# One change in three places of a two-layer attention and expert kernel: a product moved to GpSimd, feature products rewritten as row-block pairs, and a new table of steps

## Chip, cores, metric

The kernel runs on one core of one Trainium2 chip. The metric is the device time of one execution in microseconds (us). In the profile, PE is TensorE (PEld its weight loads), DVE is VectorE, ACT is ScalarE, POOL is GpSimd and SP is SyncE, which issues the DMAs.

## What is computed

Four batches of 512 tokens, width 128, go through two post-norm layers, every step with a residual and a layer norm behind it:

```python
x = ln(x + softmax_attention(x))              # layer 1: 16 heads of 8, rotary positions
# layer 1, experts: 16 experts of 64, 4 of them per token, and a shared one of 128
g = silu(einsum('th,efh->tef', x, w1_e)); u = einsum('th,efh->tef', x, w3_e)
x = ln(x + einsum('tef,ehf,te->th', g * u, w2_e, combine) + swiglu_shared(x))
# layer 2, attention: linear, with features
q, k, v = x @ Wq + bq, x @ Wk + bk, x @ Wv + bv            # 16 heads of 8
q_prime = (elu(einsum('bhsd,dm->bhsm', q, random_matrix)) + 1) / 16    # m = 32
k_prime = the same of k
x = ln(x + (q_prime (k_prime' v) / (q_prime sum(k_prime))) @ Wo + bo)
x = ln(x + x @ W.T + b + low_rank_experts(x))    # layer 2: 8 experts of rank 16, 2 per token
```

## The kernel before

Everything is float32 but the scores of layer 1. The program is written out by hand for each engine (`nc.Block()`), with semaphores; all engines walk through the same lists of steps, each taking its own part of a step (`beside_pe`, `beside_act`, `beside_dve`, `beside_pool`). An engine runs its instructions in order, so a wait on one holds all that stands behind it.

**Attention of layer 1** comes first (to about 268 us), with the steps of `slots` between its 128 half tiles. Step `combine` of batches 0 and 1 makes the tokens' expert weights `wT` and SP stores them to DRAM (`store_weights`, L358); SP brings them back spread over partitions, one tile `cw` (128x512) per pair of experts, into three buffers (`load_weights`, L362). The first `load_weights` is issued when SP has gone through all of `slots` (L402).

**The expert loop** (L778 on PE, L910 on ACT, L1248 on DVE) has 36 iterations: for each batch eight pairs of experts (p = 0 to 7) and the shared expert (p = 8, `EP`). Iteration i does on PE a `gate_e` and an `up_e` product of 128x512 (L784), then the `down` products of iteration i-1 (four of 128x128, L771), which add up over a batch in one PSUM bank. Between them ACT makes tanh of the gate (L915), DVE makes silu's product (L1254) and the product with up (`prod`, L956 from L1265), and DVE then multiplies by the expert weights `cw` into `hid` (L956 from L1270). PE waits for `hid` before `down`.

**Layer 2 beside the loop.** The list `beside[i]` holds the steps that each engine does in iteration i: PE does the first of them before `down(i-1)` and the others behind it (L785 to L791). What the loop has no room for is `layer2`, the list behind it. `chunk` sums the expert output, `norm1` normalises, `x2T` transposes; `K` and `Q` make feature blocks, `V` the values, `KV` the sums over tokens, `O`, `OT` the output, `AT` and `Y1` the projection, `norm2`, `x3T`, `lg` (gates and low-rank products), `ghT`, `Y2`, `norm3` the last part. Batch n enters the table at iteration 9(n+1), so batch 3 lies wholly in `layer2`.

**K and Q features.** Because q and k go at once through the random matrix, the products Wq·R and Wk·R (`rbd` is the random matrix repeated on the diagonal, 128x512) are made once, in steps `wR`, and their bias rows in `kb`. A bias row is split into three bf16 parts by five DVE instructions (L1146 to L1152) and laid on three partitions by three DMAs (L406). A `K` or `Q` step of one block (four of each per batch) is then one float32 product of 128x512 (L658, L664) and a bf16 product of three rows that adds the bias (L659, L665). ACT makes exp of the result less 1 (L867, L873; bias `minus1`), and DVE takes max(min(exp, 1), result) from there, with the result read from PSUM (L1159, L1175).

**Chains on DVE** (statistics, routing, low-rank gates) are generators; `step(n)` runs n of their links between other work, three (`step(1)`, `step(2)`) and `step(3)` in an expert iteration, and `finish` runs what is left before a step that needs it. GpSimd does the two small instructions of each norm's deviation (L448, L449) and adds bias rows to the residual (L454); it has no part in the loop's own work.

## Time and profile before

| | us |
|---|---|
| median of 3 runs | 527.77 (526.52 to 531.72) |
| the profiled execution | 527.63 |
| its span, first to last instruction | 525.8 |
| PE busy / weight loads | 481.0 / 232.8 |
| DVE busy | 386.0 |
| ACT busy | 224.6 |
| POOL busy | 106.5 |

Busy time is the union of an engine's instructions. A matmul's recorded end contains the run through the array, so records of PE overlap: how long a product holds PE is read from the distance between starts. A float32 product has two records and two weight loads. Many groups share L956, DVE's helper for two-input instructions, or L426, GpSimd's; they are told apart by tiles. In the trace `QS` and `KS` are also the memory of `gate_s`, `prod`, `hid` and of the exponentials (they lie over the score tiles), and `probs` that of the feature weights.

### The profile page before, as it was taken

Reading aid. Unit: us, or ns where it says so; the run is one execution under the profiler, and the core shown is the slowest. Engines: PE = TensorE matmul, PEld = TensorE weight load, DVE = VectorE, ACT = ScalarE, POOL = GpSimd, SP = SyncE. Lnnn points to the kernel's source line nnn. Section 1 sums busy time; section 2 is a strip of 40 time slices with the busy share of each in tenths; the row PEclk is TensorE's granted clock in tenths of the full one; section 3 lists DMA queues with packets and bytes.
Section 4 is the critical chain, followed back from the end, with each engine's and each line's share of the span. In section 5 each row is a group of like instructions: output and inputs, shape, how many; then the busy total and the mean of one; then the engine's idle time right before and its main releaser. Section 6 shows DMA issues by size and latency. Waiting matters only on the chain. (4 is left out here: it accounts for less than half of the span.)

```text
span 525.8 us, 7943 instructions
## 1 busy us (share of the span) xinstructions
PE 481.0 (91%) x2903; PEld 232.8 (44%) x2903; DVE 386.0 (73%) x994; ACT 224.6 (43%) x302; POOL 106.5 (20%) x101
## 2 busy tenths in 40 slices
PE   8889899999999999989979979999999999988772
PEld 3333233334333343333335545556557456545471
DVE  6398888887898888798629796974678466655553
ACT  2306657667766656656841222231332232233110
POOL 9880427006440010000100002000011001212020
PEclk9999999999999999999999999998999799879756
DMA  4854342224322333200132113112111000000000
GB/s 155 259 142 156 90 123 92 91 70 112 115 91 70 93 86 113 66 1 22 23 80 82 60 42 100 42 60 60 41 42 51 30 20 1 21 1 0 22 20 20
DMA packets 24878, 36.31 MB, mean 69 GB/s; under 512 B 2684, under 2 KB 16258, under 8 KB 24834
## 3 DMA queue, kind: packets, MB, share of 16 engines
q1 hardware_dynamic: 24840, 35.81, 23.3%
q8 instruction: 23, 0.38, 0.3%
q14 instruction: 15, 0.12, 0.1%
HBM read 24.07 MB, written 11.53 MB: 68 GB/s over the span
## 5 line engine op out<-in xcount | busy, mean ns | idle before, releaser
L1092 DVE TENSOR_REDUCE negmax<-psum 128x1 f32<-128x512 f32 x256 | 169.6, 687 | 34.0 <-PE psum L521 33.8
L805 ACT ACTIVATE probs<-psum 128x1024 f32<-128x1024 f32 x128 | 127.7, 1022 | 60.1 <-PE psum L537 57.7
L521 PE MATMUL psum<-KS,QS 125*128 125x512 bf16 x256 | 98.5, 385 | 7.4 <-DVE negmax L1092 4.1
L556 PE MATMUL psum<-probs,VA 128*32 128x256 f32 x1024 | 80.5, 390 | 0.4 <-ACT probs L805 0.4
L537 PE MATMUL psum<-QS,KS 128*128 128x512 bf16 x256 | 76.0, 380 | 0.1
L784 PE MATMUL psum<-xT,late 128*128 128x512 f32 x144 | 73.3, 634 | 0.0
L521 PEld LDWEIGHTS psum<-KS,QS 125*128 125x128 bf16 x256 | 24.5, 96 | 82.0 <-DVE negmax L1092 39.9
L448 POOL TENSOR_SCALAR var<-mv 128x4 f32<-128x4 f32 x16 | 4.3, 270 | 262.6 <-DVE mv L992 262.5
L915 ACT ACTIVATE QS<-psum 128x512 f32<-128x512 f32 x36 | 21.5, 597 | 65.2 <-PE psum L784 65.2
L771 PE MATMUL psum<-late,QS 128*128 128x128 f32 x288 | 40.6, 285 | 5.7 <-DVE QS L956 3.0
L1254 DVE SCALAR_TENSOR_TENSOR QS<-QS,psum 128x512 f32<-128x512 f32 x36 | 24.5, 680 | 26.1 <-ACT QS L915 26.1
L771 PEld LDWEIGHTS psum<-late,QS 128*128 128x128 f32 x288 | 35.9, 193 | 16.3 <-DVE QS L956 9.0
L556 PEld LDWEIGHTS psum<-probs,VA 128*32 128x32 f32 x1024 | 20.8, 108 | 38.1 <-issue 27.6
L784 PEld LDWEIGHTS psum<-xT,late 128*128 128x128 f32 x144 | 26.1, 201 | 21.4 <-issue 20.9
L537 PEld LDWEIGHTS psum<-QS,KS 128*128 128x128 bf16 x256 | 23.3, 99 | 20.1 <-issue 2.9
L426 POOL TENSOR_TENSOR res<-res,late 128x512 f32<-128x512 f32 x12 | 15.7, 1312 | 75.0 <-ACT xT L847 75.0
L426 POOL TENSOR_TENSOR rot<-rot,early 128x512 f32<-128x512 f32 x12 | 15.3, 1274 | 73.2 <-ACT rot L828 72.7
L712 PE MATMUL psum<-warm_in 128*128 128x512 bf16 x91 | 26.6, 410 | 1.5 <-POOL warm_in L478 1.5
L956 DVE TENSOR_TENSOR QS<-QS,cw 128x512 f32<-128x512 f32 x32 | 22.5, 704 | 3.8 <-DMA cw<-w_dram 3.3
L956 DVE TENSOR_TENSOR QS<-QS,psum 128x512 f32<-128x512 f32 x32 | 21.8, 683 | 2.1 <-PE psum L784 0.6
L867 ACT ACTIVATE KS<-psum,minus 128x512 f32<-128x512 f32 x16 | 11.0, 688 | 27.2 <-PE psum L659 27.2
L1175 DVE SCALAR_TENSOR_TENSOR QS<-KS,psum 128x512 f32<-128x512 f32 x16 | 10.9, 684 | 13.2 <-ACT KS L873 13.2
(148 smaller groups left out, 590.0 us busy)
## 6 DMA issues: line engine op xcount, KB each, us to landing
stack_dram<-parts SPq DMA_DIRECT2D x24, 384.0 KB, 3.3
cw<-w_dram SPq DMA_DIRECT2D x32, 256.0 KB, 3.3
KS<-stack_dram SPq DMA_DIRECT2D x16, 288.0 KB
QS<-stack_dram SPq DMA_DIRECT2D x16, 288.0 KB
late<-in_late SPq DMA_DIRECT2D x8, 346.5 KB, 4.4
res<-in_x SPq DMA_DIRECT2D x4, 256.0 KB, 3.3
w_dram<-wT SPq DMA_DIRECT2D x4, 256.0 KB, 4.4
out_y<-KS SPq DMA_DIRECT2D x4, 256.0 KB, 2.2
```

What stands on the lines that cost most here:

```text
L426: return nc.gpsimd.tensor_tensor(out=o, in0=a, in1=b, op=op)
L521: mm(sm_bank(u)[:, :], QS[b % 2][0:KROW, h, qt * P:(qt + 1) * P], KS[b % 2][0:KROW, h, :], start=True, stop=True).then_inc(sm_full, 1)
L537: last_ = mm(ps[2 * hf + j][:, :], KS[b % 2][0:KROW + 3, h, kt * P:(kt + 1) * P], QS[b % 2][0:KROW + 3, h, :], start=True, stop=True)
L556: last_ = mm(ps[6][32 * j:32 * j + 32, q], VA[b % 2][:, kt, h, :], probs[:, n % 2, j, q], start=(kt == 0 and half == 0), stop=(kt == NT - ...
L712: mm(ps[6][:, :], warm_in[:, 0:P], warm_in[:, :], start=True, stop=True)
L771: last_ = mm(bank_of(u)[:, t * D:(t + 1) * D], hid[:, i % 3, t * P:(t + 1) * P], w2, start=(p == 0 and t == 0), stop=(p == EP and t == NT ...
L784: mm(bank_of(u)[:, :], wt, xT[:, b * T:(b + 1) * T], start=True, stop=True).then_inc(fullness(u), 1)
L805: fn(probs[:, n % 2, 2 * hf:2 * hf + 2, :], psum[:, 2 * hf:2 * hf + 2, :], ACT.Exp, scale=float(DH) ** -0.5).then_inc(exp_done, 1)
L915: fn(gate_s[:, i % 2, :], bank_of(u)[:, :], ACT.Tanh, scale=0.5).then_inc(tanh_done, 1)
L956: return V.tensor_tensor(out=o, in0=a, in1=b, op=op)
L1092: V.tensor_reduce(out=negmax[:, G % 4, i:i + 1], in_=sm_bank(u)[:, :], axis=X, op=ALU.max, negate=True).then_inc(sm_free, 1)
L1254: V.scalar_tensor_tensor(out=h_, in0=h_, scalar=1.0, in1=bank_of(g)[:, :], op0=ALU.add, op1=ALU.mult)\
```

## The change

- **Experts**: `hid = prod * cw` of the 32 routed pairs is done by GpSimd, in a loop over the 36 iterations that it now walks in order with its other steps. `hid_done` is split: `routed_done` (GpSimd) and `shared_done` (DVE). DVE's `step(2)` goes with the product.
- **Features**: `wR`, `kb`, their DMAs and the bf16 bias products go. New steps `kp` and `qp`, once per batch, make the projections kT and qT (one 128x512 product each; ACT copies them to SBUF and adds the bias). A feature block then contracts over a block of heads only: K as products of 256 columns over 64 rows, Q as products of 512 columns over 32 rows, with two blocks issued together, each on its own rows of the array (`tile_position`). ACT does two instructions per block, exp and result + 1, both to SBUF, and frees the PSUM bank; DVE reads both from SBUF.
- **Table**: one list `steps`, the same for all batches, with up to 24 iterations from `chunk` to `norm3`, in place of `a_round`; what lies past iteration 35 is `layer2`, later batches first within an iteration's place.
- **Weights**: the first three `load_weights` are issued straight behind the store of batch 0 (slot 112 of 128).

The places of the steps in the new table, by iteration (batch behind the name): 0 gate2; 1 to 4 heads3; 5 attnT3; 6 proj3; 8 norm3 combine2; 9 chunk0; 10 resT3 norm1_0; 13 gate3 x2T0; 14 kp0 qp0; 15 K0 pair; 16 K0 pair, V0; 17 Q0 pair; 18 chunk1, Q0 pair, KV0; 19 O0; 20 combine3, OT0; 21 AT0; 22 x2T1; 23 kp1 qp1 Y1_0; 24 K1 pair; 25 K1 pair, V1; 26 Q1 pair, x3T0; 27 Q1 pair, KV1, lg0; 28 O1; 29 OT1; 30 AT1 ghT0; 31 x2T2 Y2_0; 32 kp2 qp2 Y1_1; 33 K2 pair; 34 K2 pair, V2; 35 Q2 pair, x3T1. Behind the loop: chunk3, Q2 pair, KV2, lg1, norm1_3, O2, OT2, AT2, ghT1, x2T3, Y2_1, kp3, qp3, Y1_2, norm3_1, K3 pair, norm2_2, K3 pair, V3, Q3 pair, x3T2, Q3 pair, KV3, lg2, O3, OT3, AT3, ghT2, Y2_2, Y1_3, norm3_2, norm2_3, x3T3, lg3, ghT3, Y2_3, norm3_3.

```diff
@@ steps beside the loop
+        steps = ((0, "chunk", 0), (1, "norm1", 0), (4, "x2T", 0), (5, "kp", 0), (5, "qp", 0), (6, "K", 0), (6, "K", 1),
+                 (7, "K", 2), (7, "K", 3), (7, "V", 0), (8, "Q", 0), (8, "Q", 1), (9, "Q", 2), (9, "Q", 3), (9, "KV", 0),
+                 (10, "O", 1), (10, "O", 0), (11, "OT", 1), (11, "OT", 0), (12, "AT", 0), (14, "Y1", 0), (15, "norm2", 0),
+                 (17, "x3T", 0), (18, "lg", 0), (21, "ghT", 0), (22, "Y2", 0), (23, "norm3", 0))
+        for n in reversed(range(NB)):
+            for at, kind, c in steps:
+                beside[PAIRS * (n + 1) + at].append((kind, n, c))
@@ when a PSUM bank is free
-                    "kb": (row_done, c + 1), "Q": (qf_done, 4 * b + c + 1), "K": (kf_done, 4 * b + c + 1),
+                    "Q": (expq_done, 4 * b + c + 1), "K": (expk_done, 4 * b + c + 1),
@@ SP
                     if kind == "combine":
                         store_weights(a)
+                        if a == 0:
+                            for j in range(CW):
+                                load_weights(j)
-            for j in range(NB * EP):
-                if j == 12:
-                    sp.wait_ge(kb_done, 2)
-                    for i in range(3):
-                        sp.dma_start(bias_stack[i:i + 1, :, :], bias_parts[0:1, :, i, :]).then_inc(ks_ld, 16)
+            for j in range(CW, NB * EP):
@@ GpSimd
+            for i in range(NB * PAIRS):
+                b, p = divmod(i, PAIRS)
+                if p < EP:
+                    j = b * EP + p
+                    pool.wait_ge(prod_done, j + 1)
+                    pool.wait_ge(cw_ld[j % CW], 16 * (j // CW + 1))
+                    if i >= 3:
+                        pool.wait_ge(down_done, i - 2)
+                    tt(hid[:, i % 3, :], prod[:, j % 2, :], cw[:, j % CW, :], ALU.mult).then_inc(routed_done, 1)
+                for s in beside[i]:
                     beside_pool(*s)
@@ PE
+                if kind in ("kp", "qp"):
+                    last_ = mm(o[:, :], c_["wk1" if kind == "kp" else "wq1"], xT[:, b * T:(b + 1) * T], start=True, stop=True)
                 if kind == "K":
-                    mm(o[:, :], tile_of(m), wkR[:, :], start=True, stop=False)
-                    last_ = mm(o[:, :], onesb[:, 0:P], bias_stack[:, 0, :], start=False, stop=True)
+                    other = ("K", b, m + 1)
+                    wait_free(pe, other)
+                    for t in range(2):
+                        for r, out_ in enumerate((o, bank_of(other))):
+                            half = slice(64 * r, 64 * (r + 1))
+                            last_ = mm(out_[:, 256 * t:256 * (t + 1)], kT[half, (m + t) * P:(m + t + 1) * P],
+                                       c_["rbd"][half, 256 * r:256 * (r + 1)], start=True, stop=True,
+                                       tile_position=(64 * r, 0))
                 if kind == "Q":
-                    mm(o[:, :], wqR[:, m * P:(m + 1) * P], xT[:, b * T:(b + 1) * T], start=True, stop=False)
-                    last_ = mm(o[:, :], bias_stack[:, 1, m * P:(m + 1) * P], onesb[:, :], start=False, stop=True)
+                    other = ("Q", b, m + 1)
+                    wait_free(pe, other)
+                    for c, out_ in ((m, o), (m + 1, bank_of(other))):
+                        rows_ = slice(HW * c, HW * (c + 1))
+                        last_ = mm(out_[:, :], c_["rbd"][rows_, c * P:(c + 1) * P], qT[rows_, :], start=True, stop=True,
+                                   tile_position=(HW * c, 0))
@@ down
-                pe.wait_ge(hid_done, i + 1)
+                pe.wait_ge(*((shared_done, b + 1) if p == EP else (routed_done, b * EP + p + 1)))
@@ ACT (Q the same with eq_, qone, qT)
+                if kind == "kp":
+                    wait_full(act, u)
+                    if a:
+                        wait_full(act, ("K", a - 1, 3))
+                    fn(kT, bank_of(u)[:, :], ACT.Identity, bias=c_["bk_col"]).then_inc(kT_done, 1)
                 if kind == "K":
...
-                    fn(ek_[:, i % 2, :], bank_of(u)[:, :], ACT.Exp, bias=minus1[:, 0:1]).then_inc(expk_done, 1)
+                    fn(ek_[:, i % 2, :], bank_of(u)[:, :], ACT.Exp)
+                    fn(kone[:, i % 2, :], bank_of(u)[:, :], ACT.Identity, bias=plus1[:, 0:1]).then_inc(expk_done, 1)
@@ DVE, an expert iteration
-                    tt(prod[:, i % 2, :], h_, bank_of(u)[:, :], ALU.mult).then_inc(prod_done, 1)
-                    step(2)
-                    dve.wait_ge(prod_done, b * EP + p + 1)
                     j = b * EP + p
-                    dve.wait_ge(cw_ld[j % CW], 16 * (j // CW + 1))
-                    tt(hid[:, i % 3, :], prod[:, i % 2, :], cw[:, j % CW, :], ALU.mult).then_inc(hid_done, 1)
+                    if j >= 2:
+                        dve.wait_ge(routed_done, j - 1)
+                    tt(prod[:, j % 2, :], h_, bank_of(u)[:, :], ALU.mult).then_inc(prod_done, 1)
                 step(3)
```

## Rows read from the trace of the kernel before

**Rows 1.** Busy time by stretch: window, PE, PEld, DVE, ACT, POOL, clock, DMA.
```profile
267.80:445.20 177.40, 167.42 (x785) 98.62 (x783) 127.24 (x340) 48.68 (x81) 13.85 (x16) 0.97 0.19 53
445.20:495.00 49.80, 43.73 (x238) 25.14 (x238) 27.68 (x110) 13.68 (x23) 8.76 (x11) 0.86 0.04 11
495.00:525.80 30.80, 16.43 (x72) 14.30 (x70) 14.78 (x69) 3.21 (x6) 4.99 (x7) 0.56 0.06 18
```

**Rows 2.** Groups by line, the expert loop alone: shapes, count, busy, mean, idle before.
```profile
L784 PE MATMUL psum<-xT,late 128*128 128x512 f32 x144 | 73.3, 634 | 0.0
L771 PE MATMUL psum<-late,QS 128*128 128x128 f32 x288 | 40.6, 285 | 5.7 <-DVE QS L956 3.0 <-DVE z L956 2.6
L956 DVE TENSOR_TENSOR QS<-QS,cw 128x512 f32<-128x512 f32 x32 | 22.5, 704 | 3.8 <-DMA cw<-w_dram 3.3
```

**Rows 3.** Waits of the loop, weight loads: us in total, times, longest.
```profile
PEld psum L771 <- DVE QS L956: 9.0, 6, 3.6
```

**Rows 4.** Timeline: an iteration with a Q step (start, duration; then a line).
```profile
345.74 1.02 PE L664 MATMUL psum<-xT,probs 128*128 128x512 f32 x2
...
346.70 0.39 PE L665 MATMUL psum<-onesb,probs 3*128 3x512 bf16 x1
347.01 0.97 PEld L771 LDWEIGHTS psum<-late,QS 128*128 128x128 f32 x8 [0.23 <-issue]
...
348.01 1.88 PE L784 MATMUL psum<-xT,late 128*128 128x512 f32 x4
```

**Rows 5.** Timeline: iterations 3 and 4 on PE, with a heads step each.
```profile
279.89 1.88 PE L784 MATMUL psum<-xT,late 128*128 128x512 f32 x4
...
283.35 1.88 PE L784 MATMUL psum<-xT,late 128*128 128x512 f32 x4
```

**Rows 6.** Timeline: the first product with a weight tile.
```profile
274.35 0.69 DVE L956 TENSOR_TENSOR QS<-QS,cw 128x512 f32<-128x512 f32 x1 [3.31 <-DMA cw<-w_dram]
...
275.10 1.16 PE L771 MATMUL psum<-late,QS 128*128 128x128 f32 x8 [2.74 <-DVE QS L956]
```

**Rows 7.** Timeline: the second bias row on DVE, and iteration 10 behind it.
```profile
307.04 0.68 DVE L1146 TENSOR_SCALAR probs<-psum 128x512 f32<-128x512 f32 x1
...
309.37 0.68 DVE L956 TENSOR_TENSOR probs<-probs 1x512 bf16<-1x512 f32 x1
...
312.87 0.97 PEld L771 LDWEIGHTS psum<-late,QS 128*128 128x128 f32 x8 [2.82 <-DVE QS L956]
```

**Rows 8.** Timeline: tanh, the two DVE products and an exp, iteration 18.
```profile
345.08 0.60 ACT L915 ACTIVATE QS<-psum 128x512 f32<-128x512 f32 x1 [0.37 <-PE psum L784]
...
345.71 0.69 DVE L1254 SCALAR_TENSOR_TENSOR QS<-QS,psum 128x512 f32<-128x512 f32 x1 [0.28 <-ACT QS L915]
...
346.49 0.69 DVE L956 TENSOR_TENSOR QS<-QS,psum 128x512 f32<-128x512 f32 x1
...
347.12 0.69 ACT L873 ACTIVATE KS<-psum,minus 128x512 f32<-128x512 f32 x1 [1.44 <-PE psum L665]
```

**Rows 9.** Timeline: GpSimd's 128x512 instructions beside DVE's with two SBUF inputs.
```profile
320.91 0.69 DVE L956 TENSOR_TENSOR QS<-QS,cw 128x512 f32<-128x512 f32 x1
320.93 1.80 POOL L426 TENSOR_TENSOR res<-res,late 128x512 f32<-128x512 f32 x1 [3.77 <-ACT xT L847]
...
393.77 1.27 POOL L426 TENSOR_TENSOR res<-res,late 128x512 f32<-128x512 f32 x1 [10.42 <-ACT xT L847]
...
394.28 1.31 DVE L956 TENSOR_TENSOR QS<-QS,cw 128x512 f32<-128x512 f32 x1
```

**Rows 10.** Timeline: eight records of four column tiles (L674), between other products.
```profile
361.22 1.06 PE L784 MATMUL psum<-xT,late 128*128 128x512 f32 x1
362.21 1.06 PE L674 MATMUL psum<-QS,KVB 128*32 128x512 f32 x8
363.21 1.16 PE L771 MATMUL psum<-late,QS 128*128 128x128 f32 x8
```

**Rows 11.** Timeline behind the loop: first step, KV of batch 2, attention's end in batch 3.
```profile
445.26 0.60 PE L646 MATMUL psum<-early,res 128*128 128x128 f32 x4
...
450.13 3.76 PE L669 MATMUL psum<-VK,KS 128*128 128x33 f32 x32
...
494.01 0.69 DVE L956 TENSOR_TENSOR attn<-psum,rt 128x512 f32<-128x512 f32 x1
```

More of the change, by code:

```diff
@@ L208, in program @@
             slots[32 * last + at].append((kind, b, 0))
-        beside = [[] for _ in range(NB * PAIRS + 12)]
+        beside = [[] for _ in range(NB * PAIRS + 25)]
         for at, kind, b, i in ((0, "gate", 2, 0), (1, "heads", 3, 0), (2, "heads", 3, 1), (3, "heads", 3, 2), (4, "heads", 3, 3),
-                               (5, "wR", 0, 0), (5, "attnT", 3, 0), (6, "wR", 0, 1), (6, "proj", 3, 0), (7, "kb", 0, 0),
-                               (8, "norm", 3, 0), (8, "combine", 2, 0), (8, "kb", 0, 1), (10, "resT", 3, 0),
+                               (5, "attnT", 3, 0), (6, "proj", 3, 0),
+                               (8, "norm", 3, 0), (8, "combine", 2, 0), (10, "resT", 3, 0),
@@ L221, in program @@
-        round_at = (4, 4, 5, 5, 5, 6, 6, 7, 7, 7, 8, 8, 9, 9, 9, 10, 10, 11, 12, 12, 12, 12)
-        for n in range(NB):
-            w = PAIRS * (n + 1)
-            for at, kind in ((0, "chunk"), (1, "norm1"), (3, "x2T")):
-                beside[w + at].append((kind, n, 0))
-            if n + 1 < NB:
-                for (kind, back, c), at in zip(a_round, round_at):
-                    if n >= back:
-                        beside[w + at].append((kind, n - back, c))
+        steps = ((0, "chunk", 0), (1, "norm1", 0), (4, "x2T", 0), (5, "kp", 0), (5, "qp", 0), (6, "K", 0), (6, "K", 1),
[3 rows of a table added]
@@ L230, in program @@
+        for n in reversed(range(NB)):
+            for at, kind, c in steps:
+                beside[PAIRS * (n + 1) + at].append((kind, n, c))
         layer2 = [s for one in beside[NB * PAIRS:] for s in one]
         del beside[NB * PAIRS:]
-        crowded = {s for one in beside for s in one} | set(layer2)
-        for n in range(last, NB + 2):
-            layer2 += [(kind, n - back, c) for kind, back, c in a_round if 0 <= n - back < NB]
+        crowded = {s for one in beside for s in one}
@@ L237, in program @@
         uses = [[] for _ in range(8)]
-        in_misc = ("rope", "val", "max", "heads", "attnT", "proj", "resT", "gate", "combine", "wR", "kb", "x2T")
+        in_misc = ("rope", "val", "max", "heads", "attnT", "proj", "resT", "gate", "combine", "x2T")
         uses[MISC] = [s for one in [[("val", 0, 0), ("max", 0, 0)]] + slots for s in one if s[0] in in_misc]
@@ L246, in program @@
             uses[5].append(("y_e", b, 0))
-        bank_for = {"K": 2, "Q": 0, "V": 4, "KV": 5, "O": 5, "OT": 5, "AT": 7, "Y1": 4, "x3T": 7, "lg": 5, "ghT": 7, "Y2": 6, "x2T": 7}
+        bank_for = {"kp": 3, "qp": 1, "K": 2, "Q": 0, "V": 4, "KV": 5, "O": 5, "OT": 5, "AT": 7, "Y1": 4, "x3T": 7, "lg": 5, "ghT": 7, "Y2": 6, "x2T": 7}
         swap = 0
@@ L502, in _ @@
                     add_row("bout_row", 0, w // 32)
-            for one in beside + [layer2]:
-                for s in one:
+            for i in range(NB * PAIRS):
[8 more added lines that the diff above has]
+                for s in beside[i]:
                     beside_pool(*s)
+            for s in layer2:
+                beside_pool(*s)
         @block.tensor
```

92 lines of the change are left out of this document (40 added, 52 removed).

## The prediction

> **What bounds the kernel now.** I read the busy time by stretch first. The kernel has three parts: attention until 267.8 us, which the change leaves as it is but for the place of three DMAs; the expert loop, 177.4 us, with PE busy for 167.4 of them; and what lies behind the loop, 80.6 us, where PE is busy for 60.2 and the granted clock falls to 0.86 and then 0.56 [rows 1]. So the loop is bound by PE's own work and the last part by a chain that goes round all engines.
>
> The groups of the loop and the timeline say what an iteration costs PE. Two float32 records of 512 columns take 1.02 us and four take 1.88 [rows 4], so each further record is 0.43 and a product of 512 columns holds PE for 0.86. `down` holds it for 0.89 (1.00 where a bf16 product stands ahead: 347.01 to 348.01 [rows 4]). An iteration with nothing beside it is therefore 1.72 + 0.89 = 2.6 us, and 36 of them are 94. I priced each step beside the loop in the same way: four transposes 0.45, eight records of 128 columns 0.9, `KV` 3.7 [rows 11], a Q or K block 1.27 (345.74 to 347.01 [rows 4]). All of it with the 36 iterations makes 155 us. The other 22 are stalls and low clock: the wait for the first weight tile (2.74), the wait behind the second bias row (2.82), DVE being late in iterations 2 to 5, the clock after the `KV` steps. The waits name DVE: PE's weight loads of `down` waited 9.0 us for it [rows 3], and an early iteration with a `heads` step takes 3.46 us [rows 5] where PE's own work is 3.0.
>
> **The change, part by part**, against the profiled execution of 527.6 us (span 525.8 and 1.8 around it; the median of the runs is 0.1 above it).
>
> *Weight tiles sooner.* DVE got its first tile at 274.35 after a wait of 3.31, and PE waited 2.74 for `down(0)` [rows 6]. The store and three loads now pass SP some 15 slots earlier, behind the last load of maxima that attention needs, so they hold up nothing; what SP then waits for is only the second `combine`. The stall goes; late next is `hid` of iteration 0 by GpSimd, about when PE comes to it. **-2.7**, bounds 0 and -3.5.
>
> *Feature steps in the loop.* 22 blocks at 1.27 go (27.9). In their place come 6 projections at 0.86 (5.2) and 11 pairs. No row has two row blocks side by side. The nearest are the column tiles: four products of 512 columns, eight records, hold PE from 362.21 to 363.21, 1.00 us, where one after the other would be 3.43; about 0.14 of it is the change to the tiled form, and as much stands ahead of it [rows 10]. If two row blocks overlap like this, a pair is 0.86 + 0.28 = 1.14; if not, 1.72 + 0.28 = 2.00. These are the bounds; I take 1.14, because the column tiles are the nearest row. 11 pairs are 12.5, and 27.9 - 5.2 - 12.5 = 10.2 saved. `x3T` of batch 1 moves into the loop, 0.45. **-9.8**, bounds -0.3 and -9.8.
>
> The Trainium skill has a rule that speaks against it: TensorEngine Tiling (Array Packing), section Key Properties, says that a change of tiling mode drains the engine. By that rule each pair pays at both ends; the trace agrees, with the 0.14 us on either side, and it is small beside the 1.4 us that a pair saves. The page TensorE: Matmul & The Clock Gate, Part 3, gives 3.07 times for four row tiles of K = 32, by which a pair would be near its lower bound; no run here shows that yet.
>
> *`wR` and `kb` gone.* Four products, 4 x 0.86, in iterations where PE had no slack: **-3.4**. On DVE each `kb` is five instructions, for the second one 307.04 to 310.05, 3.0 us, and behind it stands the wait of 2.82 in iteration 10 [rows 7]. That stall goes, though norm and the sum of batch 0 remain at that place: **-2.5**, bounds 0 and -3.5.
>
> *`x2T` one iteration later.* It stood behind a normalisation still under way; one more iteration covers it. **-1.0**, bounds 0 and -1.5.
>
> *The product on GpSimd.* DVE loses 32 instructions, 22.5 us busy [rows 2]. GpSimd's instruction of this shape with two SBUF inputs takes 1.27 [rows 9] where DVE's takes 0.69. In a bare iteration PE comes to `down(i)` 0.86 (up) + 0.89 + 1.72 = 3.5 us after the end of its gate product. The chain is 0.60 tanh, 0.69, 0.69 [rows 8], then 1.27, and some 0.1 at each of four handoffs: 3.65. So bare iterations lose 0.1 to 0.3, and those with a step beside them (29 of 36) nothing, if DVE comes in time. DVE comes sooner than before, since it was the late one in iterations 2 to 5: **-1.5** there. Against it stand the feature pairs: ACT now does four instructions of 0.60 to 0.69 [rows 8] per pair ahead of the next tanh, 2.6 us, and the next `hid` is ready some 6.0 us after the pair ends, where PE needs it after 4.3 + the step beside it (1.1 or more), or 7 where the pair stands first in its list. GpSimd takes its place in the table's order too: a deviation waits behind the product, and the product behind a bias row that waits for `x2T`; both are 1.3 us against a period of 4. I put all these new stalls at **+3**, bounds 0 and +32 (1 us for each product).
>
> *Behind the loop.* DVE's attention output of batch 3 ends at 494.7, 49.5 us after the loop's last `down` [rows 11]. Laying the new list end to end from that `down`: Q pair and `KV` of batch 2 to 5.0, `lg` 6.9, `O` and `OT` 10.1, `AT` 11.8. Then `ghT` of batch 1 waits: its gates' chain has 16 links, about 4.5 us of DVE, and the list gives it only the eight of `OT` ahead of a `finish`, so PE stands until about 16.5. `Y2`, `kp`, `qp`, `Y1` to 22.2; the K pairs at the pace of ACT (four blocks x 1.3 = 5.2), the Q pairs the same, `KV` from 33.5 to 37.2, `lg`, `O`, `OT`, and the output at 43.5. PE has more holes there than before, so I add 2 for the clock (0.86 there now [rows 1]): 45.5, -4. At the end `Y2` of batch 2 stands ahead of `Y1` of batch 3, +1.9, but the normalisation of batch 2 no longer waits beside batch 3's `lg`, -1.4. Together **-3.5**, bounds -9 and +5.
>
> Sum: -2.7 - 9.8 - 3.4 - 2.5 - 1.0 - 1.5 + 3.0 - 3.5 = -21.4, so **506.2 us**.
>
> **Rivals.**
> - *Row blocks one after the other.* For it: no row shows row tiles. Against: column tiles overlap in full. 0.86 more for each of 11 pairs in the loop, 9.5; behind the loop ACT covers all but about 1.5. 506.2 + 11 = 517.
> - *ACT or DVE takes over in feature iterations, and the clock falls with PE's thinner work.* For it: DVE's work there (two products, two maxima, ten links) is about 4.6 us against 3.7 to 4.5 of PE, and low clock is seen wherever PE streams few columns ([rows 1], last row). 0.5 us in a dozen iterations is 6, or three or four more low stretches: 512.
> - *GpSimd's product and DVE shut each other out: slower.* Where both have two SBUF inputs, DVE's product of 394.28 took 1.31 instead of 0.69, ending 0.55 after GpSimd's, and GpSimd's of 320.93 took 1.80 behind DVE's of 320.91 [rows 9]. The new product starts right behind `prod`, just where DVE goes on with links, and its maxima now have two SBUF inputs. DVE's busy time in the loop, 127.2 less 22.5 and 5.8 for `kb`, is 99; shut out for 1.27 by each of 32 products it would be 140, as much as PE's, and the two would wait in turn. It decides from 0.67 us per product (21.4 / 32), above the +3 taken; at 1.0 per product (32 - 3 = 29) the time is 535. Against: most of what DVE does behind `prod` waits for ACT anyway, and its two products read PSUM. The Trainium skill, SBUF — State Buffer, Who interferes with whom, calls this an exclusive lock for the whole instruction; the trace agrees, with the two rows named.
> - *More stalls go than I count*: of the 22 us some 12 I keep; half of them gone is 500 or less.
>
> **How the numbers follow.** Forecast 0.52 (its own range 501 to 512), ACT, DVE or clock 0.17, row blocks in turn 0.14, fewer stalls 0.10, shut out 0.07. About 1%, 5 us, is what a measurement of this kernel can tell from no change. 495 to 521 reaches over the faster case and that of the rows in turn and leaves out the slower one and the outer ends. Faster by over 1% (below 522.5) takes all but the slower case and a part of the second and third: 0.88; within 1% 0.05; slower 0.07.
>
> **What would show it.** In the profile after: no DVE wait on DMA for `cw` and `down(0)` near 272; pairs of K or Q at 1.1 to 1.2 us from start to start of what is around them (2.0 if in turn); the GpSimd product at 1.3, over 1.6 on average if shut out; the loop at 159 to 161 us and 75 to 79 behind it; PE waiting for `ghT` of batch 1 some 4 us. A loop over 170 us with PE waiting for GpSimd's product at `down` would prove the forecast wrong.

## The result, and the profile after

| | before | after |
|---|---|---|
| median | 527.77 us (20 runs, 523.61 to 531.72) | 532.66 us (20 runs, 528.73 to 536.15) |
| ratio | | 1.0108, 95% interval 1.0079 to 1.0136 |
| profiled execution / its span | 527.6 / 525.8 | 536.15 / 534.4 |
| mean granted clock of the span | 0.952 | 0.909 |

The changed kernel is 1.1% slower. The forecast was 506.2 us, so 26 us are missing. The profiled execution is the slowest of the 20, 3.5 us above the median, so its stretches are somewhat long. Medians in this document are over all runs of a kernel, while ratios leave out runs more than 1.5% above its fastest, so that the ratio of e6 rests on two of its six runs.

Busy time by stretch, with the columns of [rows 1] (window, PE, PEld, DVE, ACT, POOL, granted clock, DMA), says in which half. These are the loop and what lies behind it:

```profile
271.40:437.00 165.60, 157.11 (x794) 100.94 (x792) 118.53 (x307) 61.03 (x108) 54.61 (x50) 0.94 0.18 53
437.00:534.40 97.40, 63.89 (x306) 48.34 (x304) 41.38 (x169) 22.10 (x41) 12.27 (x16) 0.64 0.03 9
```

Against [rows 1], the loop is 11.8 us shorter (177.4 to 165.6; forecast 159 to 161). What lies behind it is 16.8 us longer (80.6 to 97.4; forecast 75 to 79). The granted clock there fell from a mean of 0.75 to 0.64. The attention in front is 3.5 us longer (267.8 to 271.3). Its own steps are not edited, and it took 268.2 to 271.1 in the kernels below, with and without the early weight loads, so nothing shows that this is part of the change.

The groups and waits of the changed kernel. First the page's group of the product on GpSimd, then two groups of the stretch behind the loop (count, busy us, mean ns, idle before), then a wait of the loop (us in total, times, longest):

```profile
L410 POOL TENSOR_TENSOR QS<-QS,cw 128x512 f32<-128x512 f32 x32 | 40.8, 1274 | 111.5 <-DVE QS L977 109.6
...
L680 PE MATMUL psum<-VK,KS 128*128 128x33 f32 x64 | 11.5, 354 | 0.0
...
L711 PE MATMUL psum<-early,KS 128*128 128x128 f32 x12 | 2.9, 385 | 9.4 <-DVE KS L977 9.4
...
PEld psum L782 <- POOL QS L410: 6.3, 8, 1.5
```

GpSimd's product takes 1.27 us each, as forecast, and is rarely shut out. PE's weight loads of `down` wait 6.3 us for it, where they waited 9.0 for DVE [rows 3]. The trouble is behind the loop: `KV` took 11.5 us for two batches (7.5 before), and `ghT` (L711) waits 9.4 us for DVE (2.6 before). PE's timeline of that stretch:

```profile
437.08 1.13 PE L672 MATMUL psum<-probs,late 32*128 32x512 f32 x4
438.14 4.50 PE L680 MATMUL psum<-VK,KS 128*128 128x33 f32 x32
443.31 1.85 PE L697 MATMUL psum<-late,xT 128*128 128x8 f32 x8 [0.67 <-DVE KVB L977]
...
446.99 3.64 PE L685 MATMUL psum<-QS,KVB 128*32 128x512 f32 x16
...
458.75 1.11 PE L711 MATMUL psum<-early,KS 128*128 128x128 f32 x4 [4.41 <-DVE KS L977]
...
480.36 7.04 PE L680 MATMUL psum<-VK,KS 128*128 128x33 f32 x32
...
502.19 1.12 PE L711 MATMUL psum<-early,KS 128*128 128x128 f32 x4 [3.42 <-DVE KS L977]
...
515.35 1.11 PE L643 MATMUL psum<-early,res 128*128 128x128 f32 x4 [5.93 <-DVE res L1021]
```

`KV` of batch 3 is 32 records as in [rows 11], where it took 3.76 us; here it takes 7.04. The low-rank gates (L697) and `O` (L685) take 1.85 and 3.64; at full clock the same sets take 1.04 and about 1.9 in runs below. The wait for `ghT` of batch 1 is 4.41, which the forecast had (4). It did not have that for batch 2 (3.42), nor 5.93 for `x3T` of batch 3.

In the loop, a K pair and, behind it, iteration 27, on PE:

```profile
324.05 1.13 PE L658 MATMUL psum<-late,probs 64*128 64x256 f32 x8
325.12 1.16 PE L782 MATMUL psum<-late,QS 128*128 128x128 f32 x8
...
383.03 1.13 PE L672 MATMUL psum<-probs,late 32*128 32x512 f32 x4
384.09 5.01 PE L680 MATMUL psum<-VK,KS 128*128 128x33 f32 x32
388.90 1.85 PE L697 MATMUL psum<-late,xT 128*128 128x8 f32 x8
390.61 2.06 PE L702 MATMUL psum<-late,xT 128*128 128x128 f32 x8
392.46 3.62 PE L795 MATMUL psum<-xT,late 128*128 128x512 f32 x4
```

A pair holds PE for 1.07 us (324.05 to 325.12): row blocks do overlap. But right behind the pairs `KV` takes 5.01, and gate and up (L795) take 3.62 us instead of 1.88. There is no gap between these rows. PE is not waiting; it is running at the lower clock. The kernel before has this too, for a shorter time: behind its `KV` of batch 0, with PE busy, gate and up took 3.64.

```profile
355.08 3.73 PE L669 MATMUL psum<-VK,KS 128*128 128x33 f32 x32
358.64 3.64 PE L784 MATMUL psum<-xT,late 128*128 128x512 f32 x4
```

### The profile page after: what moved, and what is told of

It is laid out like the page before. It is cut to its first block and busy times, and to the rows that moved or that the text cites. A ratio compares the mean times of both kernels' runs of the same rounds, so it can differ in the third digit from the quotient of the medians.

```text
span 534.4 us, 8000 instructions
## 1 busy us (share of the span) xinstructions
PE 477.8 (89%) x2911; PEld 245.0 (46%) x2911; DVE 376.6 (70%) x952; ACT 242.1 (45%) x340; POOL 145.2 (27%) x132
## 5 line engine op out<-in xcount | busy, mean ns | idle before, releaser
L514 PE MATMUL psum<-KS,QS 125*128 125x512 bf16 x256 | 100.1, 391 | 7.8 <-DMA QS<-stack_dram 3.4
L795 PE MATMUL psum<-xT,late 128*128 128x512 f32 x144 | 72.7, 629 | 0.0
L410 POOL TENSOR_TENSOR QS<-QS,cw 128x512 f32<-128x512 f32 x32 | 40.8, 1274 | 111.5 <-DVE QS L977 109.6
L795 PEld LDWEIGHTS psum<-xT,late 128*128 128x128 f32 x144 | 26.3, 203 | 21.1 <-issue 20.8
L530 PEld LDWEIGHTS psum<-QS,KS 128*128 128x128 bf16 x256 | 23.3, 99 | 20.4 <-issue 3.0
L723 PE MATMUL psum<-warm_in 128*128 128x512 bf16 x91 | 28.3, 428 | 1.5 <-POOL warm_in L462 1.5
L977 DVE TENSOR_TENSOR z<-psum,res 128x512 f32<-128x512 f32 x16 | 11.0, 689 | 24.3 <-PE psum L716 17.0
L410 POOL TENSOR_TENSOR res<-res,late 128x512 f32<-128x512 f32 x12 | 13.9, 1156 | 38.1 <-ACT xT L858 38.1
L680 PEld LDWEIGHTS psum<-VK,KS 128*128 128x128 f32 x128 | 20.9, 259 | 3.8 <-issue 3.8
```

The costliest lines, as they stand in the source:

```text
L410: return nc.gpsimd.tensor_tensor(out=o, in0=a, in1=b, op=op)
L514: mm(sm_bank(u)[:, :], QS[b % 2][0:KROW, h, qt * P:(qt + 1) * P], KS[b % 2][0:KROW, h, :], start=True, stop=True).then_inc(sm_full, 1)
L530: last_ = mm(ps[2 * hf + j][:, :], KS[b % 2][0:KROW + 3, h, kt * P:(kt + 1) * P], QS[b % 2][0:KROW + 3, h, :], start=True, stop=True)
L680: last_ = mm(cols(c, KVW), KF[:, t, c * P:(c + 1) * P], VK[:, t, c, :], start=(t == 0), stop=(t == NT - 1))
L723: mm(ps[6][:, :], warm_in[:, 0:P], warm_in[:, :], start=True, stop=True)
L795: mm(bank_of(u)[:, :], wt, xT[:, b * T:(b + 1) * T], start=True, stop=True).then_inc(fullness(u), 1)
```

## Experiments

Times are medians, ratios are to the kernel before, run on the same chip; its medians there were 527.5 to 527.9 us. "Loop" and "behind" are the two stretches of [rows 1], from the profiled run.

### The parts alone on the kernel before

**e1_weights**: the three first weight tiles loaded sooner, nothing else.

```diff
                     if kind == "combine":
                         store_weights(a)
+                        if a == 0:
+                            for j in range(CW):
+                                load_weights(j)
-            for j in range(NB * EP):
+            for j in range(CW, NB * EP):
```

> The kernel before with one edit: the first three weight tiles are loaded behind the store of batch 0. In the trace after, PE reaches down(0) without the wait of 2.74 us. If that stall was on the path (all theories say so, since the loop is bound by PE), this kernel is 2 to 3.5 us faster than before (ratio 0.993 to 0.996). Rival: DVE catches up in iterations 2 to 5 anyway and the gain is under 1 us.

523.58 us, 0.9925 [0.9891, 0.9959]. The stall goes, with 3.9 us where the sum had 2.7 with a bound of 3.5. Part of the gain is not the stall: the loop in this run has a clock of 1.00 (0.97 in [rows 1]).

**e2_table**: the new table of steps alone, with `wR` and `kb` kept as steps in it and no projections.

```diff
-        a_round = (("K", 0, 0), ("AT", 1, 0), ("K", 0, 1), ("Y1", 1, 0),
...
+        steps = ((0, "chunk", 0), (1, "norm1", 0), (4, "x2T", 0), (6, "K", 0), (6, "K", 1),
...
+        for n in reversed(range(NB)):
+            for at, kind, c in steps:
+                beside[PAIRS * (n + 1) + at].append((kind, n, c))
```

> The kernel before with the new table of steps alone (its own K and Q steps, wR and kb kept, product on DVE). Theory T, the table costs: behind the loop KV, lg and O of a batch stand next to each other, the low-rank gates have no cover, and Y1 of batch 3 waits behind Y2 of batch 2; this kernel is slower than before by 10 us or more, with the part behind the loop over 90 us (before 80.6) and more low clock than the 53 us of before. Rival R, the row blocks thin out PE's work and pull the clock down: then the table alone costs under 5 us and the low clock stays near that of before.

541.19 us, 1.0261 [1.0216, 1.0306]: 13.6 us slower. Loop and behind, busy time by stretch:

```profile
269.00:447.10 178.10, 168.36 (x789) 101.63 (x788) 130.76 (x349) 49.27 (x82) 13.90 (x19) 0.96 0.19 54
447.10:540.80 93.70, 64.05 (x304) 43.44 (x302) 41.51 (x169) 16.43 (x28) 12.53 (x16) 0.70 0.03 9
```

Nearly all of it lies behind the loop: 93.7 us for 80.6. PE's idle time there went from 20.4 to 29.7 us, its busy time from 60.2 to 64.1. The forecast laid the new list end to end and expected the stretch to get shorter.

**e8_pool_alone**: the product on GpSimd and `step(2)` gone, alone on the kernel before (the diff of the front part's "Experts").

> The kernel before with the routed product on GpSimd alone. Theory P, it costs because DVE's chains lose step(2) and are shut out behind each product: 3 to 9 us slower than before, with waits of PE for GpSimd's product and for the gates. Rival, by e3 (whose loop was 155.8 us with GpSimd's product): in the old order it costs nothing, within 2 us of before.

529.0 us, 1.0022 [0.9979, 1.0064]: nothing, either way.

### One part undone on the changed kernel

**e3_pairs_old_order**: the order of before, with each feature block beside its partner and `kp`, `qp` in front.

```diff
-        steps = ((0, "chunk", 0), (1, "norm1", 0), (4, "x2T", 0), (5, "kp", 0), (5, "qp", 0),
...
+        a_round = (("kp", 0, 0), ("AT", 1, 0), ("qp", 0, 0), ("Y1", 1, 0), ("K", 0, 0), ("K", 0, 1), ("ghT", 2, 0),
+                   ("K", 0, 2), ("K", 0, 3), ("V", 0, 0), ("norm2", 1, 0), ("Y2", 2, 0), ("Q", 0, 0), ("Q", 0, 1),
+                   ("x3T", 1, 0), ("norm3", 2, 0), ("lg", 1, 0), ("Q", 0, 2), ("Q", 0, 3), ("KV", 0, 0),
+                   ("O", 0, 1), ("O", 0, 0), ("OT", 0, 1), ("OT", 0, 0))
```

> The changed kernel with the table undone: the order of before, three batches woven into each other behind the loop, with K and Q in pairs and kp and qp in front; GpSimd product, pairs and early weight tiles kept. Theory T: this version gets what was forecast for the other parts, 505 to 513 us, with the part behind the loop at 76 to 83 us. Rival R (pairs pull the clock down) or P (the GpSimd product costs): it stays at 525 us or above, the clock behind the loop near the 0.64 of after.

**e4_dve_product**: the changed kernel with the product back on DVE.

```diff
                     tt(prod[:, j % 2, :], h_, bank_of(u)[:, :], ALU.mult).then_inc(prod_done, 1)
+                    step(2)
+                    dve.wait_ge(prod_done, j + 1)
+                    dve.wait_ge(cw_ld[j % CW], 16 * (j // CW + 1))
+                    tt(hid[:, i % 3, :], prod[:, j % 2, :], cw[:, j % CW, :], ALU.mult).then_inc(routed_done, 1)
```

> The changed kernel with the routed product back on DVE (and its step(2)). Theory T and R: the product on GpSimd is nearly neutral or a small gain, as PE waited only 6.3 us (weight loads) for it in the loop and DVE would be late as often; this kernel lies within 3 us of the changed one. Rival P, GpSimd's longer product and the shared port cost: it is 5 us or more faster than the changed one.

**e5_old_order_dve**: both edits together.

> Both costly parts undone: order of before with K and Q in pairs, product on DVE; pairs, kp and qp and the early weight tiles stay. If the table (e2: about 13 us on the kernel before) and the GpSimd product (e4: 9 us in the changed kernel) cost independently, this lies at 510 to 516 us. If the gains of e3 and e4 overlap (both fill the same stalls), it stays at 519 to 523, and what is left is the low clock behind the loop that both show (96 us there against 80.6).

| | us | ratio [95%] | loop | behind |
|---|---|---|---|---|
| after | 532.66 | 1.0108 [1.0079, 1.0136] | 165.6 | 97.4 |
| e3, old order | 522.32 | 0.9847 [0.9784, 0.991] | 155.8 | 96.0 |
| e4, product on DVE | 523.56 | 0.9884 [0.9843, 0.9924] | 157.0 | 96.0 |
| e5, both | 522.73 | 0.9902 [0.9861, 0.9942] | 155.6 | 93.4 |

Undoing either part gains 9 to 10 us; undoing both gains no more. So table and GpSimd product cost by being together, about 9 us and in the loop. What is left of the change in e5 (tiles sooner, pairs, no `wR` and `kb`) has a loop 22 us shorter than [rows 1], better than forecast, and yet gains only 5.1 us, because behind the loop it takes 93.4 us where the kernel before takes 80.6.

How table and product meet is seen in iteration 30, DVE, GpSimd and PE in the changed kernel:

```profile
408.82 1.26 POOL L410 TENSOR_TENSOR QS<-QS,cw 128x512 f32<-128x512 f32 x1 [5.04 <-DVE QS L977]
408.88 1.75 DVE L977 TENSOR_TENSOR KS<-KS,gate 128x512 f32<-128x512 f32 x1
...
410.69 1.11 PE L711 MATMUL psum<-early,KS 128*128 128x128 f32 x4 [3.44 <-DVE KS L977]
```

The gates' chain lost its links of `step(2)` with the product, so its end is still to be done when PE asks for `ghT`. Its last instruction has two SBUF inputs and starts 0.06 us after GpSimd's product: it takes 1.75 us, not 0.69. The iteration, gate start to gate start, takes 8.49 us (403.10 to 411.59), and 4.88 in e4. Counted from one iteration's tanh to the next, iteration 30 makes 4.5 of the 8.6 us between the two loops (9.38 for 4.88), and iteration 18, behind `KV` of batch 0, another 2.5 (10.48 for 8.03); there `KV` took 4.91 in the one and 3.76 in the other, which is the clock. e4 puts product and `step(2)` back together, so the links and GpSimd's longer instruction are not told apart. In the old order `ghT` comes five iterations behind `lg`, not three.

### The thin products and the clock

A K pair in the change uses 64 rows of the array at a time for each block, a Q pair 32. **e6_full_height** (on e5) and **e7_full_height_after** (on the changed kernel) contract over all 128 rows instead. The random matrix is block diagonal, so the added rows of `rbd` are zeros, and PE has more to do, not less. Two things come with it: a K pair is four records of 512 columns in place of eight of 256, and DVE writes a K block to one run of columns in place of two halves.

```diff
-                    for t in range(2):
-                        for r, out_ in enumerate((o, bank_of(other))):
-                            half = slice(64 * r, 64 * (r + 1))
-                            last_ = mm(out_[:, 256 * t:256 * (t + 1)], kT[half, (m + t) * P:(m + t + 1) * P],
-                                       c_["rbd"][half, 256 * r:256 * (r + 1)], start=True, stop=True,
-                                       tile_position=(64 * r, 0))
+                    for r, out_ in enumerate((o, bank_of(other))):
+                        last_ = mm(out_[:, :], kT[:, (m + r) * P:(m + r + 1) * P], c_["rbd"], start=True, stop=True)
...
-                        last_ = mm(out_[:, :], c_["rbd"][rows_, c * P:(c + 1) * P], qT[rows_, :], start=True, stop=True,
-                                   tile_position=(HW * c, 0))
+                        last_ = mm(out_[:, :], c_["rbd"][:, c * P:(c + 1) * P], qT, start=True, stop=True)
```

> e5 with one edit: K and Q blocks as products over all 128 rows (the zeros of rbd multiplied too, so two blocks take 1.72 us of PE instead of 1.07, 16 times, some 10 us more PE work), same two-block steps and evacuation. Theory R, thin products let the clock fall: low clock behind the loop goes from about 70 us back towards 40 and this kernel is as fast as e5 or faster. Rival: rows of the array do not matter for the clock, the time is 5 to 10 us longer than e5 and the low clock the same.

> The changed kernel with the same edit (full-height products; its table and GpSimd product kept). Theory R: at or below 533 us with less low clock (after: 20.5 us in the loop, 69.5 behind). Rival: 538 to 543.

**e9_thin_twice**: the changed kernel with each thin product issued twice into the same place, so that a pair streams on few rows for about as long as in e7 (1.93 us, there 1.72).

```diff
-                    for t in range(2):
+                    for t in (0, 1, 0, 1):
...
-                    for c, out_ in ((m, o), (m + 1, bank_of(other))):
+                    for c, out_ in ((m, o), (m + 1, bank_of(other))) * 2:
```

> The changed kernel with each K and Q product of few rows issued twice (same result): a pair holds PE for about 1.9 us, as long as the full-height pair of e7 (1.72), but with 64 or 32 rows of weights per product. If what matters for the clock is how long the array streams, this is like e7: about 522 to 526 us, low clock near 50 us in all behind the loop. If the rows in use matter, it is slower than the changed kernel: 537 to 545, low clock as in after (90 us) or more.

| | us | ratio [95%] | pair on PE | loop, clock | behind, clock |
|---|---|---|---|---|---|
| after | 532.66 | 1.0108 [1.0079, 1.0136] | 1.07 | 165.6, 0.94 | 97.4, 0.64 |
| e7, full height | 522.07 | 0.9922 [0.9888, 0.9956] | 1.72 | 159.4, 1.00 | 90.9, 0.72 |
| e9, thin twice | 542.17 | 1.0302 [1.0246, 1.0357] | 1.93 | 173.2, 0.94 | 97.1, 0.69 |
| e5 | 522.73 | 0.9902 [0.9861, 0.9942] | 1.06 | 155.6, 0.99 | 93.4, 0.64 |
| e6, full height | 518.2 | 0.9741 [0.9642, 0.9841] | 1.72 | 161.2, 0.98 | 84.5, 0.74 |

With 0.65 us more work in every pair the kernel is 10.6 us faster (4.5 on e5). By the ratios it is 1.9% and 1.6%, and the intervals of each pair don't meet. Iteration 27 of these profiled runs is a place where they differ. Busy time by stretch, first from the pairs of batch 1 up to `KV`, then from `KV` on; the changed kernel, with PE busy for the whole of both windows:

```profile
369.20:384.09 14.89, 14.89 (x82) 9.07 (x81) 13.10 (x28) 8.77 (x16) 5.60 (x6) 1.00 0.12 37
384.09:396.00 11.91, 11.91 (x55) 9.84 (x54) 4.32 (x17) 3.66 (x7) 0.96 (x1) 0.59 0.06 22
```

The same two in e7, and PE's rows there:

```profile
366.20:383.15 16.95, 16.95 (x73) 10.22 (x72) 13.82 (x28) 9.70 (x18) 6.36 (x6) 1.00 0.10 33
383.15:393.00 9.85, 9.85 (x77) 7.40 (x75) 6.09 (x19) 3.60 (x7) 1.43 (x3) 1.00 0.08 27
```
```profile
381.44 1.88 PE L667 MATMUL psum<-probs,late 128*128 128x512 f32 x4
383.15 3.66 PE L674 MATMUL psum<-VK,KS 128*128 128x33 f32 x32
386.64 1.04 PE L691 MATMUL psum<-late,xT 128*128 128x8 f32 x8
...
388.51 1.88 PE L789 MATMUL psum<-xT,late 128*128 128x512 f32 x4
```

And in e9:

```profile
387.66:399.00 11.34, 11.34 (x53) 10.01 (x52) 3.33 (x14) 3.46 (x7) 0.11 (x1) 0.57 0.07 25
```
```profile
385.75 1.99 PE L673 MATMUL psum<-probs,late 32*128 32x512 f32 x8
387.66 5.63 PE L682 MATMUL psum<-VK,KS 128*128 128x33 f32 x32
```

Three kernels, the same steps in the same order, PE busy without a gap in each. In the two with thin pairs the granted clock falls to the lower level (1.2 GHz) while `KV` runs, in e9 too, whose pairs stream as long as the full ones. In this run of e7 it stays at 2.4 GHz. But full height does not always hold it: e12 and e13 below do exactly what e7 does in the loop, and in both the clock fell right behind this `KV`, with PE busy. From `KV` on in e12:

```profile
382.14:392.53 10.39, 10.39 (x53) 8.44 (x52) 4.05 (x16) 3.00 (x6) 0.17 (x1) 0.67 0.08 25
```
```profile
382.14 3.73 PE L677 MATMUL psum<-VK,KS 128*128 128x33 f32 x32
385.68 1.86 PE L694 MATMUL psum<-late,xT 128*128 128x8 f32 x8
...
389.23 3.46 PE L792 MATMUL psum<-xT,late 128*128 128x512 f32 x4
```

The loops of e12 and e13 took 165.6 and 165.5 us, as long as that of the changed kernel, and e7's 159.4; e10 below, with the loop of the changed kernel, took 162.5. So the 6.2 us that e7 gained in the loop are largely luck of the run, and in the old order the loop's clock is no better with full height (0.98) than without (0.99). What both pairs of kernels show is the stretch behind the loop: 97.4 to 90.9 us with the clock going from 0.64 to 0.72, and 93.4 to 84.5 with 0.64 to 0.74. The mean clock of whole runs agrees: 0.909 to 0.923 in the 20 runs of the changed kernel, 0.940 to 0.949 in the 12 of e7.

So the thin form lowers the clock. Streaming longer does not mend it: e9 is 20 us slower than e7, though its clock behind the loop (0.69) lies between that of the changed kernel and that of e7. Whether it is the rows in use, or the tiled form and K's shorter records that come with them, no run tells apart. `KV` itself has 33 columns per record and pays most for a low clock: 3.66, 5.01, 5.63, and 7.04 where it lies wholly in the low stretch.

### The clock alone

**e10_fill_after** (on the changed kernel) and **e11_fill_best** (on e6) add bf16 products of zeros, whose result nothing reads, on PE behind the loop, where PE would wait or has only small products.

```diff
+            def fill(count):
+                ...
+                    for _ in range(count):
+                        mm(ps[bank][:, :], warm_in[:, 0:P], warm_in[:, :], start=True, stop=True)
...
             for s in layer2:
                 beside_pe(*s)
+                fill(after_step.get(s, 0))
```

> The changed kernel with about 110 bf16 filler products (zeros, 128x512, 0.22 us each, as in its start) behind the loop alone: two after each quarter of KV, and where PE waits for the gates, the norm and copies. If the low clock behind the loop is what the time goes into, low clock there falls from 69.5 us to under 20 and the part behind the loop from 97.4 to 78 to 86 us, although PE has 24 us more work: 516 to 524. If the clock is only a sign of waits that would be there anyway, the time stays at 530 or rises.

> e6 (order of before, full-height products, product on DVE, early weight tiles) with filler products of the same kind behind the loop. If the clock carries the time as in e10: 504 to 511 us, the part behind the loop at 72 to 78 us. If not: 518 or above.

e10: 528.25 us, 0.9991 [0.9945, 1.0037]. That is 4.4 us off the changed kernel with 77 more records, less than expected; behind the loop it took 91.2 us, where 78 to 86 were expected. The clock behind the loop rose from 0.64 to 0.80 only: in the feature pairs of batch 3, which got no fillers, it stayed low. e11: 510.07 us, 0.9677 [0.9626, 0.9728]. That is 8.1 us off the median of e6, but only 0.6% by the ratios, whose intervals overlap. Behind the loop (84.5 in e6):

```profile
427.80:507.00 79.20, 60.37 (x356) 40.64 (x355) 43.40 (x179) 22.81 (x41) 13.30 (x18) 0.91 0.05 14
```

The low clock costs by itself: the same steps on all engines, more work on PE, and a shorter stretch, in three pairs of kernels: 97.4 to 91.2 us (e10), 84.5 to 79.2 (e11) and 90.9 to 84.2 (e7 to e13 below). With e15 below this is the fastest version of the case, 3.2% faster than the kernel before and 4.2% than the changed one (510.07 / 532.66).

### What the table and GpSimd cost once the clock is high

**e12_end_order** is e7 with the last steps (`Y1`, `ghT`, `norm2`, `Y2`, `x3T`, `norm3`) put in the order of before.

> e7 (changed kernel, full-height products) with the last steps in the order of before: Y1 of batch 3 and its norm ahead of ghT and Y2 of batch 2. In after PE waits 5.9 us for x3T of batch 3 behind 3.4 us for the gates of batch 2. If this piece of the table is on the path, 5 to 7 us less than e7: 515 to 517. If the gates of batch 2 are needed by DVE's chains anyway: within 2 us of e7.

524.83 us, 0.9954 [0.9913, 0.9994], and e7 has 522.07. Behind the loop it is 87.5 for 90.9, but its loop, in which nothing differs from e7's, had a clock of 0.96 for 1.00 and was 6.2 us longer. No gain shown; the run settles nothing about the end's order.

The last three runs keep full-height products and fillers and change only table and product. **e13_table_full_fill**: e7 and the fillers of e10. **e14_table_full_fill_dve**: e13 and the edit of e4. **e15_best_gpsimd**: e11 with the product on GpSimd.

> The changed kernel (new table, GpSimd product) with the K and Q products over all 128 rows and filler products behind the loop. If the low clock is the main loss, both steps add up (-10.6 and -4.4 on the changed kernel when done alone) and the time is 514 to 519, with at most 80 to 86 us behind the loop. If the new table costs by itself, through chains that wait whatever the clock is, it stays at 518 or above and at least 9 us above e11_fill_best (510.1).

> e13_table_full_fill with the routed product back on VectorE; only the table still differs from e11_fill_best, beside where the fillers stand. If the table costs only where the clock is low, 508 to 512. If the table costs by itself: 514 or more, with VectorE named in the waits behind the loop. From e4 against the changed kernel (-9) the GpSimd product should be worth 5 to 9 us here if it costs with the new table at any clock.

> e11_fill_best with the routed product on GpSimd: the old order, so by e3 against e5 and by e8 it should change nothing, 508 to 512. If GpSimd's product costs in any order once the clock is high, 514 or more.

| | us | ratio [95%] | loop | behind |
|---|---|---|---|---|
| e11: old order, DVE | 510.07 | 0.9677 [0.9626, 0.9728] | 159.4 | 79.2 |
| e15: old order, GpSimd | 510.10 | 0.9678 [0.9649, 0.9707] | 159.0 | 79.2 |
| e14: new table, DVE | 511.94 | 0.9725 [0.9666, 0.9784] | 157.1 | 82.6 |
| e13: new table, GpSimd | 518.98 | 0.9849 [0.9789, 0.9908] | 165.5 | 84.2 |

Behind the loop, e14 and then e13:

```profile
426.70:509.30 82.60, 63.52 (x369) 41.23 (x373) 41.18 (x169) 22.10 (x40) 12.20 (x16) 0.93 0.03 10
```
```profile
433.70:517.90 84.20, 65.14 (x369) 41.90 (x373) 41.19 (x169) 22.10 (x40) 12.20 (x16) 0.91 0.03 10
```

With the clock held up, the table costs 3.4 us behind the loop and gives 2.3 in it: 1.9 us in sum, within the intervals (the fillers of the two, 54 and 71 records, stand at different places). So of the 13.1 us that it costs behind the loop in e2, 3.4 are left. That the rest is the clock's is the likeliest reading, but not shown alone, since e11 and e14 also have pairs. The GpSimd product costs nothing in the old order, at either clock (e8, e3 against e5, e15 against e11), and 7.0 us with the new table (e13 to e14; 9.1 from the changed kernel to e4). Of the 8.4 us between the loops of e13 and e14, 6.0 stand in iterations 30 and 31 (tanh to tanh) and 1.7 in 27 and 28, where e13 has more of the low clock. Its place is the same as before: the `ghT` of iteration 30, here in e14, where PE waits 0.36 us and not 3.44:

```profile
400.92 0.66 PE L708 MATMUL psum<-early,KS 128*128 128x128 f32 x4 [0.36 <-DVE KS L983]
```

## Why the prediction failed

**Weight tiles sooner, -2.7.** Right in mechanism and a little small: e1 gives -3.9. The loop's first `down` starts 4.6 us after the loop (271.37 to 275.94), 7.3 before.

**Feature steps in the loop, -9.8.** Right. The one unknown price was taken at the correct end: 1.14 for a pair, measured 1.07. The Trainium skill, TensorE: Matmul & The Clock Gate, Part 3, has row tiles overlap; this case agrees, 1.07 us against 1.72 for the two blocks at full height. The rival of row blocks in turn is refuted. That of more stalls gone holds for the loop alone (e5's is 22 us shorter).

**`wR` and `kb` gone, -3.4 and -2.5; `x2T` later, -1.0; DVE relief, -1.5.** No run has these alone. With the tiles and the pairs they made -22 us of loop in e5 (177.4 to 155.6), against -20.9 forecast for all the terms of the loop without new stalls. Iteration 10, where the wait behind the bias row stood, went from 5.89 to 3.05 us. In e8, which keeps `kb` but takes the product off DVE, it took 4.38, so only a part of the stall was the bias row's.

**New stalls from GpSimd's product and ACT, +3 (0 to +32).** Measured +7 to +9, all of it together with the table: after against e4, e13 against e14. The rival in which both engines shut each other out is refuted as it was put (1.27 us a product, no cost in e8, e3 and e15). What was overlooked is smaller and sits mainly in one place, iteration 30: the links that `step(2)` no longer runs, in a table that asks for `ghT` three iterations behind `lg`. That it is the links is read from the rows of that iteration and was not tried alone. With the product on DVE the loop is shorter than forecast (159 to 161): 157.0 in e4.

**Behind the loop, -3.5 (bounds -9 and +5).** This is the step that failed: +16.8, far outside its bounds. Up to the attention output of batch 3 it took 61.0 us from the last `down` (437.1 to 498.1), and 45.5 were forecast; from there to the end 36.3, and 31.6 were forecast. I laid the steps of the new list end to end at the durations of rows at full clock, and added 2 us for the clock. With the 3.5 in the attention and 5.6 in the loop, and less the 3.5 by which the profiled run is above the median, the 20.3 us that this stretch lies above its forecast (97.4 for 77.1) make up the 26.

How the stretch divides on PE says what kind of time it is (us; fillers, 14.9 and 19.1, are counted with the rest):

| behind the loop | own products, about | rest | clock |
|---|---|---|---|
| before | 60.2 | 20.4 | 0.75 |
| after | 63.9 | 33.5 | 0.64 |
| e11: old order, DVE, full height, fillers | 45.5 | 33.7 | 0.91 |
| e14: new table, DVE, full height, fillers | 44.4 | 38.2 | 0.93 |

Against the kernel before, 13.1 of the 16.8 us are time in which PE does nothing. But e14 has the same steps in the same order with no fewer holes, and its own products take 19.5 us less, although its pairs are wider. At that clock the stretch is 5.5 us above the forecast; the other 14.8 go with the low clock, waits and products together. The runs put three things in the place of the 2 us, which don't add up simply:
- The thin products bring the clock down: with the table, 6.5 us behind the loop (after against e7), and in it 6.2 in one run and nothing in two (e12, e13); in the old order, 8.9 behind it (e5 against e6), less the 5.6 that the wider pairs cost in the loop.
- The table makes holes and brings the clock down too. It puts `KV`, `lg`, `O` and `OT` of a batch back to back, all small products, and leaves the gates' chain with nothing beside it. Alone that is 13.1 us behind the loop (e2), where the clock goes from 0.75 to 0.70 and 9.2 of the 13.1 are PE's idle time. It is hardly anything on top of thin products (e5 to e4: 2.6 behind, 0.8 in sum) and 1.9 at a high clock.
- The waits of PE for DVE's gates and norms (4.41, 3.42, 5.93) are real. But a hole filled with products of zeros costs less than an empty one: the fillers alone took 6.2 us off this stretch (e10), and 6.7 with full height (e7 to e13).

The second rival had this mechanism ("the clock falls with PE's thinner work") with a price of 6 us, three or four more low stretches, and a chance of 0.17. The mechanism was right and the size was not, and its warrant was weak: the row it named (low clock "wherever PE streams few columns") is a stretch in which PE is also idle for 14.4 of 30.8 us, while `KV`, with 33 columns, ran at full clock in the kernel before (3.76). It was priced as a few stretches in the loop, and the stretch behind it, which already had a clock of 0.56 in its last part [rows 1], was left with +2. That row was a warning: here a part whose clock was already low lost more by thinner work than it gained by less work. The range (495 to 521) failed for the same reason: bounds of -9 and +5 were given to a sum of 60 us of PE work of which each microsecond can double.

The Trainium skill, TensorE: Matmul & The Clock Gate, section HAM oscillation, names waits of PE between groups of products as what brings the clock down. The trace of the changed kernel agrees in the wait of 5.93 before `x3T` of batch 3, in the midst of which the clock fell:

```profile
509.40:512.00 2.60, 0.02 (x1) 0.00 (x0) 2.41 (x12) 0.00 (x0) 0.49 (x2) 1.00 0.00 0
513.00:515.35 2.35, 0.00 (x0) 0.00 (x1) 2.04 (x8) 0.00 (x0) 1.06 (x2) 0.50 0.18 57
```

It doesn't cover iteration 27, where PE was busy for all of 26.8 us (369.20 to 396.00) and the clock still fell, nor the same place in e12, nor the one behind `KV` in the kernel before. Whoever looks only for waits would call these places safe.

**Open.** How much of e2's cost is the small products back to back and how much the chain without cover was not separated; e12 tried the end's order, and its loop's clock hid the answer. What in the thin form lowers the clock (rows in use, tiled form, shorter records) was not told apart. Of the four profiled kernels with this table and full height, the clock stayed up in iteration 27 in e7 alone; why it fell in e12 and e13, with the same loop, is not known.

## What to carry to other kernels

Row tiling shortens a product and can still lose, as it did here: where the neighbours are small products, compare with the full-height form in the whole kernel, and read the granted clock of the stretches behind it. Take more than one run for a stretch: the same loop took 159.4 us in e7 and 165.6 in e12, by the clock alone. Before adding terms laid end to end, read the clock of the stretch: below 1, its durations aren't those of the rows elsewhere. When two engines share a chain's links, moving one instruction moves the place where links are run; look at every step that asks for the chain's end.

## What was not expected of the hardware

- The granted clock fell with PE busy throughout: 1.00, then 0.59 behind row-tiled float32 pairs, 0.57 with these issued twice, 1.00 in e7 and 0.67 in e12 and e13 with all 128 rows. Over whole runs the form tells: 0.909 to 0.923 thin, 0.940 to 0.949 at full height.
- `KV`, 32 records of 33 columns with a weight load each, goes from 3.66 to 7.04 us between the clocks, nearly the full factor of two, although a record has only 33 columns; gate and up of 512 columns went from 1.88 to 3.62.
- Adding 54 products of zeros behind the loop made that stretch 5.3 us shorter (84.5 to 79.2, e6 to e11).
- GpSimd's product of 128x512 in float32 took 1.26 to 1.31 us in all 32 places, and cost the kernel nothing in the old order (e15 against e11: 510.10 and 510.07).
